# Second layer's closing: decoder and mean in one product of 64 output rows, the two halves in two banks

## The reference, cut to what matters

```python
x = x + _L2_conv_ref(_gn(x), ...)
# in _L2_conv_ref, for each of 1024 pixels, with 256 model channels:
h = jnp.einsum('bdl,de->ble', u, W_enc) + b_enc
g = g[..., :D_MODEL] * jax.nn.sigmoid(g[..., D_MODEL:])
h = _layernorm(h + g, ln_gamma, ln_beta)      # over the 256 model channels
out = h @ W_dec + b_dec                       # 256 -> 32 channels
```

## Time and profile before

| | |
|---|---|
| median of 3 runs | 1698.12 us (1697.15 to 1698.41) |
| profiled execution | 1698.67 us, of which the span 1696.9 us |
| PE busy | 1339.8 us, 4164 instructions |
| DVE busy | 1006.1 us, 1809 |
| ACT busy | 541.9 us, 870 |
| POOL busy | 1180.7 us, 1187 |

### The profile page before, as it was taken

The page is one execution under the profiler, slowest core; times in us unless marked ns, Lnnn a source line. Parts: engine busy times, 40 slices in busy tenths (PEclk is TensorE's granted clock), DMA queues, the critical chain, the costliest instruction groups (busy, mean ns, idle before and its releaser), DMA issues.

```text
span 1696.9 us, 13775 instructions
## 1 busy us (share of the span) xinstructions
PE 1339.8 (79%) x4164; PEld 611.3 (36%) x4164; DVE 1006.1 (59%) x1809; ACT 541.9 (32%) x870; POOL 1180.7 (70%) x1187
## 2 busy tenths in 40 slices
PE   8778566999849958879969848789849644898797
PEld 7543233444324413324334313334224211343345
DVE  4546765544662479943655588845433794445785
ACT  2122212323332331243423412342413304244345
POOL 1477777756777777777777778777777777777700
PEclk9889877999969979989979979989869876899899
DMA  7233223421322222322332223322221112222000
GB/s 254 64 82 84 79 66 84 118 61 56 92 78 73 65 57 77 90 75 56 86 97 59 62 62 84 92 64 70 61 76 53 50 53 59 81 64 68 22 10 16
DMA packets 109609, 123.06 MB, mean 73 GB/s; under 512 B 49952, under 2 KB 85856, under 8 KB 109408
## 3 DMA queue, kind: packets, MB, share of 16 engines
q0 software_dynamic: 36864, 75.57, 15.8%
q1 hardware_dynamic: 71712, 43.40, 10.0%
q10 hardware_dynamic: 960, 3.21, 0.5%
HBM read 101.89 MB, written 9.01 MB: 65 GB/s over the span
## 4 chain that ended last, share of the span: by engine, by line
PE 37%; POOL 25%; DVE 20%; issue 10%; ACT 5%; DMA 2%; SPq 1%; DVEq 0%; POOLq 0%; ACTq 0%
POOL gt L1042 25%; PE bank L1991 7%; PE bank L2004 6%; DVE rb L1742 5%; PE bank L1941 4%; PE bank L1905 4%; PE bank L1901 3%; PE bank L1915 3%; DVE gt L1626 3%; PE bank L1974 2%; DVE he L1524 1%; PE bank L2027 1%; DVE gt L1628 1%; PE bank L2048 1%; PE bank L1805 1%
## 5 line engine op out<-in xcount | busy, mean ns | idle before, releaser
L1042 POOL DMA_INDIRECT gt<-corner_table,idx x1152 | 1155.8, 1003 | 422.3 <-issue 347.3
L1991 PE MATMUL bank<-u,wk 128*128 128x512 f32 x512 | 240.4, 614 | 3.7 <-DMA u<-sqb 3.7
L2004 PE MATMUL bank<-yg,wts 128*128 128x512 f32 x512 | 234.3, 602 | 0.4 <-DVE rb L1682 0.2
L1626 DVE TENSOR_TENSOR gt<-gt,bank 128x1152 f32<-128x1152 f32 x128 | 172.6, 1349 | 88.2 <-DMA gt<-corner_table,idx 87.1
L1905 PE MATMUL bank<-xg,w_sb 128*128 128x512 f32 (+1 forms) x256 | 135.3, 612 | 45.1 <-DVE xg L1515 23.3
L1961 PE MATMUL bank<-cst,sm 128*128 128x128 f32 x384 | 75.9, 313 | 118.1 <-DVE sm L1634 117.9
L1668 DVE SCALAR_TENSOR_TENSOR tg<-tg,ae 128x512 f32<-128x512 f32 x64 | 44.1, 692 | 198.2 <-ACT ae L1218 198.2
L1742 DVE SCALAR_TENSOR_TENSOR rb<-xp,par,rb 128x1024 f32<-128x1024 f32 x124 | 155.0, 1291 | 0.0
L1991 PEld LDWEIGHTS bank<-u,wk 128*128 128x128 f32 x512 | 97.3, 197 | 121.7 <-issue 114.7
L1524 DVE SCALAR_TENSOR_TENSOR he<-he,bank 128x512 f32<-128x512 f32 (+1 forms) x128 | 83.0, 651 | 92.0 <-PE bank L1905 88.8
L2004 PEld LDWEIGHTS bank<-yg,wts 128*128 128x128 f32 x512 | 95.2, 192 | 111.5 <-issue 109.4
(11 more groups left out here) (283 smaller groups left out, 1512.5 us busy)
## 6 DMA issues: line engine op xcount, KB each, us to landing
gt<-corner_table,idx POOLq DMA_INDIRECT x1152
tb<-gate_of_token SPq DMA_DIRECT2D x56, 256.0 KB, 4.9
u<-sqb SPq DMA_DIRECT2D x48, 128.0 KB, 2.8
corner_table<-tb SPq DMA_DIRECT2D x36, 128.0 KB, 2.7
w_sb<-w ACTq DMA_DIRECT2D x6, 512.0 KB, 7.1
xp<-x_patch SPq DMA_DIRECT2D x4, 512.0 KB, 4.4
X<-x SPq DMA_DIRECT2D x1, 1536.0 KB, 9.2
out<-X SPq DMA_DIRECT2D x6, 256.0 KB, 2.2
```

Of the source, the lines that this page charges most:

```text
L1042: pool.indirect_dma_start(gt[:, t % GRING, k].rearrange("p a c -> p (a c)"), None, corners, bass.IndirectOffsetOnAxis(ap=idx[s % 2][:, j, ...
L1626: ch.then(tt(rows, rows, share.unsqueeze(2).to_broadcast([P, 4 * KK, C]), ALU.mult))
L1991: op = mm(psum[b][:, :], wk[:, t, d], u4[:, g, at:at + HALF], start=t == 0, stop=t == JJ - 1 and n > 0)
L2004: op = mm(psum[B2.bank(*name)][:, :], w_glu[:, k, col + d * P:col + (d + 1) * P], yg[:, c % 2, k], start=k == 0, stop=k == NB2 - 1)
```

## The change

The weights `wdp` get 96 columns per block: 32 of 1/256 (the mean), 32 of the decoder, 32 of 1/256 again. One product of 64 output rows then gives a unit's mean and its decoder result: the first half of the pixels takes columns 32 to 96 (decoder, mean), the second columns 0 to 64 (mean, decoder). The results of the first half lie in one bank, those of the second in another ("both2", 0 and 1), so that every strip of 32 rows has one decoder result in one of the two banks (`place_of`) and the mean in the strip beside it. The squares' product comes last, in a third bank. ACT squares the means strip by strip, one instruction for each unit. DVE multiplies both banks in place, all rows each, and then adds each unit's strip into X, one instruction for each unit. The weights' four new blocks are written once by four small DVE operations.

```diff
-def strip(s, c):
+def place_of(s, c):
     n, g = unit(s, c)
-    return g ^ n * len(GROUPS[s][close_of(s, c)])
+    images = GROUPS[s][close_of(s, c)]
+    return (2 * images.index(g) if len(images) > 1 else 2) + n
+def base_of(s, c):
+    return place_of(s, c) // 2 * 2
...
-                use(third, *((x, *k) for x in ("mu", "sq", "dec")))
+                use(third, ("both2", *k, 0), ("both2", *k, 1), ("sq", *k))
...
-        wdp = sb("wdp", [P, NB2, C])
+        wdp = sb("wdp", [P, NB2, 3 * C])
...
+        def mean_rows(s, c):
+            return rows([place_of(s, c) ^ 1])
...
# ACT
             def l2_close(s, q):
-                r = both(s, q)
-                b = B2.bank("mu", s, q)
-                B2.filled(act, "mu", s, q)
                 act.wait_ge(S["x2_added"], FROM + closed(s, q))
-                act.activation(musq[r, :], psum[b][r, :], ACT.Square).then_inc(free[b], 1)
+                for n in range(2):
+                    b = B2.bank("both2", s, q, n)
+                    B2.filled(act, "both2", s, q, n)
+                    for c in closing(s, q):
+                        if unit(s, c)[0] == n:
+                            op = act.activation(musq[rows([place_of(s, c)]), :], psum[b][mean_rows(s, c), :], ACT.Square)
+                op.then_inc(S["musq_ready"], 1)
...
# DVE
-                tt(wdp[:, :, :], wg2[:, :, :],
+                for d in range(NB2):
+                    for at in (0, 2 * C):
+                        ch.did(ts(wdp[:, d, at:at + C], con("mean256"), 1.0, None, ALU.mult))
+                tt(wdp[:, :, C:2 * C], wg2[:, :, :],
...
             def l2_end(s, q):
-                r, o = rows(GROUPS[s][q]), rows(beside(s, q))
+                r = both(s, q)
                 dve.wait_ge(S["rstd2_ready"], closed(s, q) + 1)
-                B2.filled(dve, "dec", s, q)
-                b = B2.bank("dec", s, q)
-                ch.did(tt(musq[r, :], psum[b][r, :], var2[r, :], ALU.mult))
+                banks = [psum[B2.bank("both2", s, q, n)] for n in range(2)]
+                for n in range(2):
+                    B2.filled(dve, "both2", s, q, n)
+                    ch.did(tt(banks[n][r, :], banks[n][r, :], var2[r, :], ALU.mult))
                 ch.wait()
-                tt(var2[r, :], psum[b][o, :], var2[o, :], ALU.mult).then_inc(free[b], 1)
-                x0, x1 = (X[r, s, n * HALF:(n + 1) * HALF] for n in range(2))
-                stt(out=x0, in0=musq[r, :], scalar=dconst[r, 0:1], in1=x0, op0=ALU.add, op1=ALU.add)
-                B2.read(dve, "dec", s, q)
-                stt(out=x1, in0=var2[r, :], scalar=dconst[r, 0:1], in1=x1, op0=ALU.add, op1=ALU.add)\
-                    .then_inc(S["x2_added"], 1)
+                for n in range(2):
+                    for c in closing(s, q):
+                        half, g = unit(s, c)
+                        if half == n:
+                            x = X[rows((g,)), s, n * HALF:(n + 1) * HALF]
+                            op = stt(out=x, in0=banks[n][rows([place_of(s, c)]), :], scalar=dconst[rows([place_of(s, c)]), 0:1],
+                                     in1=x, op0=ALU.add, op1=ALU.add)
+                    if n == 0:
+                        op.then_inc(free[B2.bank("both2", s, q, 0)], 1)
+                op.then_inc(S["x2_added"], 1)
+                dve.wait_ge(S["x2_added"], FROM + closed(s, q) + 1)
+                dve.sem_inc(free[B2.bank("both2", s, q, 1)], 1)
...
# PE
-                for kind, weight, src in (("mu", None, rb), ("sq", None, sqb), ("dec", wdp, rb)):
-                    b = B2.bank(kind, s, q)
-                    B2.vacant(pe, kind, s, q)
+                for n in range(2):
+                    b = B2.bank("both2", s, q, n)
+                    B2.vacant(pe, "both2", s, q, n)
                     for d in range(NB2):
                         for c in cs:
-                            g = strip(s, c)
-                            lhs = weight[:, d] if weight is not None else con("mean256")[:, 0:C]
-                            op = mm(psum[b][g * C:(g + 1) * C, :], lhs, src[:, slot(s, c), d], start=d == 0,
-                                    stop=d == NB2 - 1)
+                            if unit(s, c)[0] == n:
+                                at = base_of(s, c) * C
+                                op = mm(psum[b][at:at + 2 * C, :], wdp[:, d, (1 - n) * C:(3 - n) * C], rb[:, slot(s, c), d],
+                                        start=d == 0, stop=d == NB2 - 1)
                     op.then_inc(full[b], 1)
+                b = B2.bank("sq", s, q)
+                B2.vacant(pe, "sq", s, q)
+                for d in range(NB2):
+                    for c in cs:
+                        op = mm(psum[b][rows([place_of(s, c)]), :], con("mean256"), sqb[:, slot(s, c), d], start=d == 0,
+                                stop=d == NB2 - 1)
+                op.then_inc(full[b], 1)
```

More of the change, by code:

```diff
@@ L293, in closed @@
     return sum(len(GROUPS[i]) for i in range(s)) + q
-def strip(s, c):
+def place_of(s, c):
     n, g = unit(s, c)
-    return g ^ n * len(GROUPS[s][close_of(s, c)])
-def beside(s, q):
-    return [strip(s, c) for c in closing(s, q) if unit(s, c)[0]]
+    images = GROUPS[s][close_of(s, c)]
+    return (2 * images.index(g) if len(images) > 1 else 2) + n
+def base_of(s, c):
+    return place_of(s, c) // 2 * 2
 def last_of(s, images):
@@ L803, in build @@
             xpad_ready rows_ready om_ready mask_ready idx_ready smp_ready relu_done
-            u_ready glu_done sq_ready ln2_ready rstd2_ready x2_added
+            u_ready glu_done sq_ready ln2_ready rstd2_ready musq_ready x2_added
             xp3_ready y3_ready diag_ready diag_used ysq_ready rstd3_ready yz_ready yn_ready x3_ready fold_in out_done
@@ L829, in both @@
         def both(s, q):
-            return rows([strip(s, c) for c in closing(s, q)])
+            return rows([place_of(s, c) for c in closing(s, q)])
+        def mean_rows(s, c):
+            return rows([place_of(s, c) ^ 1])
         def span(a, halves):
@@ L1674, in l2_z @@
                 if c >= GI:
-                    B2.filled(dve, "dec", s, close_of(s, c - GI))
+                    for half in range(2):
+                        B2.filled(dve, "both2", s, close_of(s, c - GI), half)
                     dve.wait_ge(S["sq_ready"], (s * 8 + closing(s, close_of(s, c - GI))[-1] + 1) * NB2)
@@ L1688, in l2_var @@
                 B2.filled(dve, "sq", s, q)
-                B2.read(dve, "mu", s, q)
+                dve.wait_ge(S["musq_ready"], closed(s, q) + 1)
                 tt(var2[r, :], psum[b][r, :], musq[r, :], ALU.subtract).then_inc(free[b], 1)
             def l2_end(s, q):
-                r, o = rows(GROUPS[s][q]), rows(beside(s, q))
+                r = both(s, q)
                 dve.wait_ge(S["rstd2_ready"], closed(s, q) + 1)
-                B2.filled(dve, "dec", s, q)
-                b = B2.bank("dec", s, q)
-                ch.did(tt(musq[r, :], psum[b][r, :], var2[r, :], ALU.mult))
+                banks = [psum[B2.bank("both2", s, q, n)] for n in range(2)]
+                for n in range(2):
+                    B2.filled(dve, "both2", s, q, n)
+                    ch.did(tt(banks[n][r, :], banks[n][r, :], var2[r, :], ALU.mult))
                 ch.wait()
-                tt(var2[r, :], psum[b][o, :], var2[o, :], ALU.mult).then_inc(free[b], 1)
-                x0, x1 = (X[r, s, n * HALF:(n + 1) * HALF] for n in range(2))
-                stt(out=x0, in0=musq[r, :], scalar=dconst[r, 0:1], in1=x0, op0=ALU.add, op1=ALU.add)
-                B2.read(dve, "dec", s, q)
-                stt(out=x1, in0=var2[r, :], scalar=dconst[r, 0:1], in1=x1, op0=ALU.add, op1=ALU.add)\
-                    .then_inc(S["x2_added"], 1)
+                for n in range(2):
[10 more added lines that the diff above has]
+                dve.sem_inc(free[B2.bank("both2", s, q, 1)], 1)
             def l3_head(s):
```

## The result

The changed kernel takes 1709.1 us (median of six runs, 1703.41 to 1711.51), the kernel before 1697.63 in the same rounds. The ratio is 1.0061 with a 95% interval of 1.0046 to 1.0076: 10.4 us slower, 8 to 13. The forecast was 8.8 us, 1707.

What follows compares the result with a forecast made beforehand. POOL's gathers were taken as the kernel's clock, with work free unless POOL waits for it. Terms 0.6 + 1.5 + 3.3 + 1.8 + 0.1 + 1.5 = 8.8 us gave a median of 1707 us, range 1701 to 1713.

Steps and rivals of the forecast that it cites:

- Which closings cost: Of nine closings, the first, second, sixth and last two are exposed; the four others, covered by POOL, cost nothing.
- covered after all: Rival: the middle closings are hidden, only decoder weights and tail count, 2.2 us, 1700 us; chance 0.13.
- The sign that I named for it: POOL's waits before the gathers near 701 and 717 us grow by about 4.8 us in all.
- 64-row products side by side: PE in a full closing: two 64-row tiles overlap, 1.72 us a product, so PE gains nothing.
- The rival at 1718: 64-row products run one after the other, 3.44 us more per full closing, +10.3 us exposed; chance 0.08.
- The decoder's weights: Four small DVE operations writing the weight blocks add 0.15 to 0.2 us each, +0.6 us, passed on in full.
- First closing: At 484 to 498 us: DVE's six operations at the end instead of four, +1.5 us; the square's move costs nothing.
- Between the first two closings: From 498 to 598 us: no added cost; PE clock shifts taken as zero and put into the range.
- Second closing: At 598 to 610 us: square's later place 1.7, tile-size switch 0.1, DVE's end 1.5, together +3.3 us.
- Sixth closing: At 1324 us: again 3.3 us, of which 1.5 is free as slack before the gather, leaving +1.8 us.
- Eighth closing: Image 2, at 1584 us: the square comes about level with what already held `var`, +0.1 us.
- Last closing: At 1648 us: ACT decides; the second Square begins a product later, so the logarithm comes +1.5 us later.

Runs made afterwards that it cites:

- hidden4: Kernel before with the new form only in the third, fourth, fifth and seventh closings, plus the four weight blocks: 1695.98 us, ratio 0.9993.
- exposed5: Kernel before with the new form only in the first, second, sixth, eighth and ninth closings, plus the four weight blocks: 1706.69 us, ratio 1.0058.
- sqlast: Kernel before with only the squares' product moved to third place in each closing: 1700.31 us, ratio 1.0013.
- mimic: Kernel before with squares' product third, two extra DVE operations per four-unit closing and the four weight blocks: 1706.31 us, ratio 1.0050.
- first2: Kernel before with the new form only in the first two closings, plus the four weight blocks: 1702.1 us, ratio 1.0035.
- adds: Kernel before with only two extra DVE operations in each four-unit closing: 1704.88 us, ratio 1.0043.
- last1: Kernel before with the new form only in the last closing, at 1648 us: 1700.59 us, ratio 1.0017.
- run 16: Not a follow-up run: a verb and a count, 16 of the 32 passes that `var` waits for in the sixth closing.
- warm2_after: Changed kernel with extra PE matmuls in idle time after the first closing and at two further places: 1702.75 us, ratio 1.0030 to the kernel before.
- warm_after: Changed kernel with 36 extra PE matmuls in the idle time after the first closing: 1707.35 us, ratio 1.0058 to the kernel before.
- warm2 pair: Kernel before and changed kernel, each with extra PE matmuls after the first closing and at two further places: 1695.10 and 1702.75 us.

## Why the prediction held, step by step

- **Which closings cost.** Right, and shown: hidden4 is level with before, exposed5 with after. The rival "covered after all" has fallen, and so has a price for every closing. The sign that I named for it came only in part: of the two POOL waits before 701 and 717 us, which were to grow by 4.8 together, the first grew by 3.0 and the second not at all. The rest of the waiting came earlier, at 624 and 692 us.
- **64-row products side by side.** Right: 16 passes of 64 rows run as eight pairs. In the sixth closing, at full rate throughout, the steps between pairs are 0.43 us, the first 0.48, and the one into the square's product 0.53: the change of tile size costs 0.10, as taken from the earlier trace rows. The rival at 1718 has fallen. In the second closing the first product's 5.81 us is the lower clock.
- **The decoder's weights**, +0.6: 0.35, over-sized. From 256.31 to 256.66 the four begin 0.09 us apart, less than the 0.15 to 0.2 taken. From the step's first operation to the decoder's product it is 1.61 us before (253.53 to 255.14) and 2.10 after (254.56 to 256.66); the other 0.14 is the second operation of `tg`, whose length changes from execution to execution (0.23 before, 0.37 here, 0.44 in sqlast, which has no blocks). In exposed5 and mimic it is 0.23, and the step takes 1.96, again 0.35 more. The price is in the second column, which scatters by more.
- **First closing**, +1.5: right (2.85 to 4.38 us from the first multiplication to the end of the last addition), and DVE's wait for itself, 0.11 us here and 0.19 at the second, was not seen ahead. The five operations by their starts: 0.61, 0.72, 0.75, 0.78, 0.76 us. The multiplication into the bank takes 0.70, as chosen.
- **Between the first two closings**, 0: wrong by 0.9 to 1.1 us. The prediction named PE's clock and put it into the range. The runs show that it isn't a scatter around zero: a later end of a closing lengthens PE's idle time and with it the slow stretch behind. DVE's wait there is 0.8 to 1.2 us longer in after, first2, exposed5, adds and mimic, and not longer in sqlast, hidden4 and last1; and the surplus falls from 1.0 to 0.1 us where extra matmuls keep the clock up.
- **Second closing**, +3.3: 3.7 (DVE's wait +2.18, of which 1.8 is the products' new order and the rest their slower clock; the end of the closing +1.52), and the 0.19. So from the first closing to G54 it is 6.5 us where the steps gave 4.8.
- **Sixth closing**, +1.8: over-sized, 0.6 at POOL (1352.18). The term took the wait for `var` of before plus 1.72; but there the closing had run 16 of the 32 passes that `var` waits for at the lower clock, and after it ran at full rate: first product to `var` 5.40 us before, 5.58 after. In exposed5 the wait is 1.3 above the usual, in mimic 1.2.
- **Eighth closing**, +0.1: from its first product to `var` 7.60 us before and 7.85 after.
- **Last closing**, +1.5: 1.57 to the logarithm (4.85 to 6.42 us from its first product), which came 3.5 us behind the first Square's end and not 3.8. Behind it came 1.0 more in this execution. "All that follows is a serial chain" had left out a link: the bank of a closing's first product used to be free after ACT's Square, and is now held to the first addition. Of eight passes of the third layer there, which ran in one piece before, the last two wait for that addition, and the 18 filling passes behind them (L1823; the same 18 took 2.27 us before) run at the lower clock:
```profile
1667.87 1.87 PE L2109 MATMUL bank<-w_sb,wts 32*128 32x512 f32 x2 [2.76 <-DVE X L1716]
1669.66 4.21 PE L1823 MATMUL bank<-cst 128*128 128x128 f32 x18
```
  But the wait is 2.76 us in every execution with the new form here, and what follows differs. From the last addition to the end it is 39.2 us in after, exposed5 and warm2_after, and 37.5 or 37.6 in last1 and warm_after (with 3.69 and 3.74 for the 18); the old form has 37.4 to 38.2. warm_after has the whole change, so the 1.0 is no fixed part of its price. What decides between the two lengths stays open.

The forecast was 1.6 us low in the ratio. Against it the middle took 1.7 us more and the tail 1.1, the sixth closing 1.2 less: 1.6 (the smaller errors at the blocks and the eighth closing aside). So the forecast was right in which closings cost, in what a closing costs and in what stays free; that the errors of its parts offset each other so far is luck, since 1.0 of the tail comes and goes between executions and the sixth closing was over-sized. Faster gathers did come (5.3 us less in their sum), but executions of the other kernels have 1144 to 1154 us too, the level ones among them, so that is scatter and no effect of the change.

## What to carry to other kernels

Ask of each instance of a repeated step whether something waits behind it, and price only those: here four of nine were free, and the experiment that splits the instances tells more than any on the operations. When a step delays the work on which TensorE waits, the delay need not be the whole price; look at the granted clock behind the idle time, since the next products may run at half rate longer (here 1.0 us more behind a closing that ended 1.6 us later). A product that serves two results at once also ties their banks together: ask when each bank was released before, and who waits for it.

## What the runs showed of the hardware

- VectorE's multiplication from a bank into the same bank (128x512) takes 0.70 us, like one into SBUF; two into different banks, without a wait, start 0.61 us apart. Four additions with 32 rows each, every one in another quadrant than the one before, start 0.75 to 0.78 apart; the two of the kernel before, each 0.74 long and both from and into the same quadrants, started 0.67 apart. The Trainium skill (VectorE: DVE Perf Modes, Two Vector instructions with no wait between them) says that such an instruction is held until the earlier ones have finished; the trace agrees.
- A wait of VectorE for its own last operation, with the semaphore increment behind it, costs 0.11 and 0.19 us (0.15 and 0.22 instead of 0.03 before the next operation, at the first and the second closing). The Trainium skill (VectorE: DVE Perf Modes, The DRAIN you can't avoid) found no cost for a semaphore after each of eight copies; there is one here, where the waiting instruction is not the next operation but one that releases a bank, and the measurement decides.
- Two TensorE tiles of 64 rows lose nothing against four of 32; a step is 0.43 us with either, and the switch between the sizes costs 0.10 us once (0.53).
- Behind 36 filling matmuls in an idle stretch the next products ran at 2.4 GHz (3.70 us for eight passes instead of 5.40), in the kernel before and in the changed one, at a granted clock of 1.00. The stretch to the second closing was then no longer lengthened by the closing's later end (97.80 and 97.92 us in the warm2 pair, against 99.50 and 100.55 without the extra matmuls).
